# The running maxima of an attention in f16, turned by products with an f16 identity

## The reference

```python
scores = einsum('bhid,bhjd->bhij', q, k)
rel = einsum('bhid,pd->bhip', q, rel_key)
bias = take_along_axis(rel, clip(j - i + p - 1, 0, p - 1), axis=3)
logits = where(j <= i, (scores + bias) * hd ** -0.5, -inf)
out = einsum('bhij,bhjd->bhid', softmax(logits, axis=-1), v)
```

## Time and profile before

| | us |
|---|---|
| median of three runs | 3905.11 (3901.54 to 3906.79) |
| the profiled execution | 3913.09 |
| its span, first to last instruction | 3911.5 |
| PE busy | 3411.8 (87%) |
| PEld busy | 2951.2 (75%) |
| DVE busy | 2384.1 (61%) |
| ACT busy | 1407.0 (36%) |
| POOL busy | 1270.0 (32%) |

### The profile page before, as it was taken

One profiled execution on the slowest core, in us unless ns is written; L12 is line 12 of the kernel. 1 busy time (PEld: TensorE's weight loads), 2 busy tenths in 40 slices (PEclk: granted clock), 3 DMA queues, 4 the chain that ended last, 5 costly groups with the idle time before them and its releaser, 6 DMA issues. The chain is left out here.

```text
span 3911.5 us, 164368 instructions
## 1 busy us (share of the span) xinstructions
PE 3411.8 (87%) x72480; PEld 2951.2 (75%) x72480; DVE 2384.1 (61%) x4876; ACT 1407.0 (36%) x1690; POOL 1270.0 (32%) x1501
## 2 busy tenths in 40 slices
PE   6964999999989999999899999989999999189980
PEld 4534888888878888888788888878888888168770
DVE  5853567777256666753566777346567771276774
ACT  1320233344512334354123334522233446155551
POOL 1004433222354332234443322344333211222556
PEclk8986999999989999999899999999999999599995
DMA  3764101000311010003111000131000000544664
GB/s 112 207 169 115 34 24 35 28 26 19 91 55 41 29 37 26 19 29 109 37 39 37 29 19 26 45 97 35 29 29 29 22 13 11 176 128 141 191 181 131
DMA packets 249778, 259.11 MB, mean 66 GB/s; under 512 B 104041, under 2 KB 192333, under 8 KB 248957
## 3 DMA queue, kind: packets, MB, share of 16 engines
q1 hardware_dynamic: 227964, 205.30, 17.9%
q0 software_dynamic: 21120, 43.42, 3.6%
HBM read 151.36 MB, written 95.99 MB: 63 GB/s over the span
## 5 line engine op out<-in xcount | busy, mean ns | idle before, releaser
L887 DVE TENSOR_TENSOR att_acc<-att_pm,att_acc 128x512 f32<-128x512 f32 x1920 | 1267.1, 687 | 542.0 <-PE att_pm L1006 265.3
L967 ACT ACTIVATE att_pt<-att_ps 128x1024 f32<-128x1024 f32 x560 | 573.7, 1025 | 1611.9 <-PE att_ps L998 1603.3
L998 PE MATMUL att_ps<-att_qz,table_z 128*128 128x64 f16 x8960 | 729.7, 194 | 8.9 <-issue 8.8
L995 PE MATMUL att_ps<-att_qx,table_x 68*128 68x64 f16 x8960 | 732.1, 195 | 4.7 <-issue 4.6
L970 ACT ACTIVATE att_pt<-att_ps 128x1024 f32<-128x1024 f32 x528 | 515.3, 1022 | 354.1 <-PE att_ps L1006 351.9
L998 PEld LDWEIGHTS att_ps<-att_qz,table_z 128*128 128x128 f16 x8960 | 621.8, 99 | 8.9 <-issue 8.7
L995 PEld LDWEIGHTS att_ps<-att_qx,table_x 68*128 68x128 f16 x8960 | 619.3, 99 | 8.2 <-issue 7.9
L1088 PE MATMUL att_po<-att_pt,att_vn 128*32 128x128 f32 x17408 | 603.3, 280 | 1.8 <-issue 1.6
L991 PE MATMUL att_ps<-att_qs,att_kn 113*128 113x64 f16 x8960 | 455.5, 194 | 76.5 <-DMA att_qs<-s_m 71.3
L1088 PEld LDWEIGHTS att_po<-att_pt,att_vn 128*32 128x32 f32 x17408 | 452.1, 111 | 88.5 <-issue 73.1
L991 PE MATMUL att_pm<-att_qs,att_kn 113*128 113x64 f16 x8672 | 444.9, 195 | 81.3 <-POOL att_qx L759 46.9
(11 more groups left out here) (209 smaller groups left out, 4073.8 us busy)
## 6 DMA issues: line engine op xcount, KB each, us to landing
att_qe<-s_q SPq DMA_DIRECT2D x256, 128.0 KB
moe_xs<-s_h SPq DMA_DIRECT2D x78, 256.0 KB
s_y<-moe_y SPq DMA_DIRECT2D x78, 256.0 KB
s_v<-prj_vx SPq DMA_DIRECT2D x32, 512.0 KB, 3.9
att_vn<-s_v SPq DMA_DIRECT2D x64, 256.0 KB, 3.5
att_qs<-s_q SPq DMA_DIRECT2D x128, 66.0 KB
prj_x<-in_x POOLq DMA_DIRECT2D x16, 512.0 KB, 4.3
att_kn<-s_k SPq DMA_DIRECT2D x128, 64.0 KB, 2.5
```

Of the source, the lines that this page charges most:

```text
L887: dve.tensor_tensor(held, got, held, ALU.max).then_inc(bank_done, 1)
L967: act.activation(pt[:, k % 2, :, t * 64:t * 64 + 64].rearrange("p h (x c) -> p x h c", x=2), ps[t][:, :, :].rearrange("p x (h c) -> p x h ...
L995: last = pe.matmul(groups[:, :, g], keep["table_x"][:, y:y + P], qx[0:G * D + G, s, x * (XQ // G) + g], start=False, stop=(g == XQ // G - ...
L998: last = pe.matmul(groups[:, :, g], keep["table_z"][:, y:y + P], qz[:, s, x * (XQ // G) + g], start=False, stop=(g == XQ // G - 1), skip_g ...
```

## The change

`acc` becomes f16. The first write of a block no longer copies but takes the maximum with -60000, so that the masked scores (sums of products of -30000) stay within f16. The turns become ordinary matmuls with `acc` as the stationary operand and an f16 identity as the moving one, in place of the transposing form with the f32 identity; the result is f32 in PSUM as before. GpSimd makes the second identity. Nothing else changes: the plan, the semaphores, the buffers and their numbers are the same.

```diff
+LOWEST = -60000.0
@@ phase_modulation, gpsimd
                 pool.memset(keep["ident"][:, :], 0.0)
+                pool.memset(keep["ident_h"][:, :], 0.0)
...
                 pool.wait_ge(pool_step, 1)
+                pool.affine_select(out=keep["ident_h"][:, :], in_=keep["ident_h"][:, :], compare_op=ALU.not_equal,
+                                   fill=1.0, base=0, pattern=[[-1, P]], channel_multiplier=1)
@@ phase_attention
-        acc = a.sb("acc", [P, 2, H, P])
+        acc = a.sb("acc", [P, 2, H, P], F16)
@@ vector, bank
-                            dve.tensor_copy(held, got).then_inc(bank_done, 1)
+                            dve.tensor_scalar(held, got, LOWEST, None, ALU.max).then_inc(bank_done, 1)
@@ tensor, bank
-                            last = pe.transpose(full[:, g * P:(g + 1) * P], acc[:, n % 2, 4 * r + g, :], keep["ident"][:, :])
+                            last = pe.matmul(full[:, g * P:(g + 1) * P], acc[:, n % 2, 4 * r + g, :], keep["ident_h"][:, :],
+                                             start=True, stop=True, skip_group_check=True)
@@ KEEP
+    "ident_h": ([P, P], F16),
```

## The result

| | kernel before | changed kernel |
|---|---|---|
| median | 3905.7 us (9 runs) | 3892.9 us (9 runs) |
| ratio, 95% interval | | 0.9965 (0.9952 to 0.9978) |
| profiled execution | 3913.1 us | 3899.8 us |
| span | 3911.5 us | 3898.2 us |

I had predicted 3850. The change brings 13 us where 55 were forecast. A repeat on another chip gave 0.9966.

The account below looks back on a forecast made before the run. TensorE was taken to bound the attention, busy 2776.3 of 2930 us. Turns save 62 us, waits take back 7, VectorE, GpSimd and clock count nothing: 55 us off 3905.1 gives 3850, range 3820 to 3880.

Parts of the forecast that it names:

- The price of a turn: On TensorE in the attention: an f16 turn takes 57 ns, a bank of four 0.23 us instead of 0.48.
- A: Turns on TensorE: stationary load isn't hidden under 128 columns; 84 ns a turn, 0.34 us a bank, 3875; chance 0.10.
- E: Turns on TensorE: four-byte data or transposing form doesn't set the 0.12 us, pitch stays, 3905; chance 0.03.
- The term of 62 us: TensorE's turns: 256 banks save 0.25 us each, 64 us, less 2 us for the 12 banks outside the stretch.
- VectorE's and GpSimd's edits at nothing: Running maxima and first writes on VectorE, added mask work on GpSimd: cost nothing, covered by spare time.
- What waits take back: TensorE's weight loads held by VectorE's reduction: half of 58 places lose 0.25 us, 7 us off the gain.
- the bank at 1206.67: Four turns on TensorE starting at 1206.67: 0.48 us to the next instruction, 0.12 us a turn, called typical.
- The clock at nothing: TensorE's granted clock in the attention, mean 0.97: nothing in the sum, 10 us either way in the range.
- Rival D: TensorE's clock falls more often as a larger share is idle; slower, 3938 at a grant of 0.94; chance 0.04.
- Rival C: TensorE's clock falls less often with ordinary products; grant 0.98 instead of 0.97, another 29 us, 3821; chance 0.07.
- The DMA wait keeps the saving: TensorE's waits for the maxima's DMA: the row is ready earlier by what the turns save, so the saving stays.
- Rival B: VectorE becomes the pace around the turns, half of all banks lose their 0.25 us; gain 31 us, 3874; chance 0.10.

Follow-up runs that it names:

- Twofold turns: The changed kernel with each of the four f16 products of a turn bank issued twice in a row: 3906.4 us, 0.9991 of the kernel before.
- the pair with both absorbers reduced: Kernel before and changed kernel, both with earlier turns, seven eighths of each running maximum and half of each reduction left out: 3741.8 and 3699.0 us.

## Why the prediction was wrong

- **The price of a turn: right.** 0.22 us a bank against 0.23 forecast; interpolating between the products of 64 and 256 columns held. Rivals A and E are out. The 81 ns of the Trainium skill ("TensorE: Matmul & The Clock Gate", "Back-to-back issue gap") isn't borne out by this trace: four turns with their loads start within 0.22 us, 55 ns each. The term of 62 us was at most 2 or 3 us too large.
- **VectorE's and GpSimd's edits at nothing: right.** Twofold turns gave 0.9991; the running maximum takes 686 ns (687 before), the first write 687 as before.
- **What waits take back: this step failed.** I put 7 us, from the 58 places where a weight load waited for the reduction L889. These did grow by about 7 us (22.4 + 16.4 + 10.6 to 24.9 + 18.4 + 12.9). But I had left out the waits for the running maximum (28.1 and 26.9 us in 178 places in the rows above), which were longer in sum, and that each of the three buffers frees in VectorE's order, so that any time TensorE saves lets it arrive earlier at the next of these. All waits of loads for VectorE together grow by 29 us; by the distances of starts, 17 of the 60 us are lost to waits that were already due at the end of the turns, and another 18 in later waits, where I had 7 for both. The three rows were also not the largest three, as I said: a row of 15.3 us for the DMA of the row of maxima stood between them. The clue was in the rows I chose: the bank at 1206.67 had a distance of 0.48 where four turns need 0.44 to 0.47. Its last turn took 120 ns to the next start where the two before it took 109 each: it ended in a short wait of the kind I was looking for, and I read it as work.
- **The clock at nothing: mis-sized.** Rival D had the mechanism, and it works here on a smaller scale: 0.940 to 0.935, 10.6 us by the distances of starts. I had argued that the waits before the falls have other causes than the turns and stay. The longest, for the row of maxima, did stay, but TensorE is at half clock for longer all the same, and every pair of runs shows a lower median clock for the shorter turns. Rival C, the opposite sign, is out. The Trainium skill says that transposing products do not count as busy in the same way ("TensorE: Matmul & The Clock Gate", "Part 4: PE-mode transpose"). The run with each product issued twice bears on it: with ordinary products in place of the transposing ones, for about the same time, the clock was the same (0.939 and 0.940 in the profiled executions, 160 us at half clock against 164). At this share of TensorE's work no difference shows.
- **The DMA wait keeps the saving: right in size, for another reason.** The wait stayed at 57 to 59 us in sum, so no more than 2 us of the saving went there. But not because the turns are earlier: the row is queued behind GpSimd's expansion, which starts when TensorE has finished the block before, and so moves with TensorE.
- **Rival B** (3874) was the nearest in mechanism: waits for VectorE that take half of the saving back. It was still too small by itself and needs D's part beside it.
- **Does the account close?** The sum 60 - 29 - 8.5 leaves 22 where 13 were measured. The rows of idle time are too coarse for it; distances of starts are not. Both traces hold all 68608 products of the attention in the same order, so each distance from one start to the next can be compared with its partner. The turns are 43 us shorter. The other products that ran at full clock in both traces are 17.6 us longer, some 16 of it at waits for VectorE, and those at half clock in either are 10.6 us longer. That is 14.8 us less for the attention; the profiled executions differ by 13.3. In the pair with both absorbers reduced the turns are 60 us shorter, the other two parts 7.1 and 2.2 us longer: 50.6, and these executions differ by 50.3. What stays open is why one bank is released late and its neighbour not; no run takes that apart.

## What to carry to other kernels

An engine that is busy 95% of a stretch and has few long waits isn't free of coupling: where it shares a few buffers with an engine that empties them in order, ask for each instruction saved which buffer it will reach earlier and whether that one is free then. Price a shortened step by the distance of starts in several places, and compare with the pitch of like instructions; a distance above the pitch is a wait already there. Where the gain doesn't come, first remove the longest fixed waits (here by planning the row of maxima earlier, 69 us for a changed constant): the clock and the later savings both profit.

## What the runs showed of the hardware

- An f16 product of 128 columns with its own 128-column load has a pitch of 55 ns; the f32 transposing one has 109 ns, the same as an f16 product of 256 columns (111), and often 141 for the first of a bank.
- A running maximum from PSUM takes the same 0.69 us whether the other operand and the result are f16 or f32.
- Products of no use in the waits raised the grant of the next 10 us from 0.66 to 0.83 and cut the half-clock time of the attention from 181 to 147 us; the median was 10 us lower with more work, though the intervals overlap.
- Of 114 us of added TensorE work 59 showed in the time, of 60 us removed 13; with both absorbers reduced 42.
